# A two-layer transformer on one core: one list of rows per expert for a whole layer, 71 blocks in place of twice 39

## The reference, cut to what matters

```python
x = x + tanh(g_xattn[0]) * xattn0(layernorm(x), ctx)      # 8 heads of 64
x = x + tanh(g_ffn[0])   * ffn0(layernorm(x))             # silu(a)*b experts, with biases
x = x + tanh(g_xattn[1]) * xattn1(layernorm(x), ctx, ctx) # 16 heads of 8
x = x + tanh(g_ffn[1])   * ffn1(layernorm(x))             # gelu experts
# an expert layer: scores -> top 2 of 8 -> weights; y = sum of weight * expert(x) over the two
```

## Time and profile before

| | us |
|---|---|
| median of 3 runs | 836.9 (834.84 to 841.38) |
| span of the profiled execution | 772.1 |
| between that span and the median | 64.8 |
| granted TensorE clock, mean over the span | 0.945 |

### The profile page before, as it was taken

The page is one execution under the profiler, slowest core; times in us unless marked ns, Lnnn a source line. Parts: engine busy times, 40 slices in busy tenths (PEclk is TensorE's granted clock), DMA queues, the critical chain, the costliest instruction groups (busy, mean ns, idle before and its releaser), DMA issues.

```text
span 772.1 us, 17182 instructions
## 1 busy us (share of the span) xinstructions
PE 646.2 (84%) x4648; PEld 591.0 (77%) x4648; DVE 574.2 (74%) x2005; ACT 434.4 (56%) x1195; POOL 476.3 (62%) x693
## 2 busy tenths in 40 slices
PE   6889888988875789898978998898788875879896
PEld 5668777887765779888967787788788875868886
DVE  3369788988786678997977988987967753845763
ACT  2456565664444657666757776686566553434451
POOL 4034347776577777885563445675566577677771
PEclk9999999999798999999979999999999998999998
DMA  9646667544443235443713632532524013344646
GB/s 258 183 110 170 171 175 180 148 122 130 107 135 92 84 105 145 120 130 110 197 57 99 137 92 77 138 107 70 118 84 87 25 54 94 113 119 127 177 140 180
DMA packets 132633, 95.90 MB, mean 124 GB/s; under 512 B 32148, under 2 KB 120756, under 8 KB 132476
## 3 DMA queue, kind: packets, MB, share of 16 engines
q1 hardware_dynamic: 114844, 69.16, 35.1%
q0 software_dynamic: 9088, 19.68, 7.9%
q10 hardware_dynamic: 8608, 5.99, 2.7%
HBM read 55.09 MB, written 44.10 MB: 128 GB/s over the span
## 4 chain that ended last, share of the span: by engine, by line
PE 35%; DVE 28%; issue 11%; ACT 9%; POOL 8%; DMA 5%; SPq 2%; DVEq 1%; ACTq 0%; POOLq 0%
PE banks L1063 10%; PE banks L927 4%; DVE row_max L1297 4%; PE banks L1082 4%; DVE prob L1300 3%; POOL x_rows L1719 3%; DMA y_rows<-y_sb,result_at 3%; POOL y_rows L1726 2%; PE banks L809 2%; SPq L721 2%; PE banks L871 1%; DVE x_res L1569 1%; DVE row_sum L1351 1%; ACT xm L1177 1%; DMA v_rows<-vo 1%
## 5 line engine op out<-in xcount | busy, mean ns | idle before, releaser
L1726 POOL DMA_INDIRECT y_rows<-y_sb,result_at x156 | 151.4, 970 | 58.0 <-issue 31.2
L1063 PE MATMUL banks<-xb,up 128*128 128x128 f32 x936 | 140.2, 288 | 19.5 <-DVE hidden L1545 8.4
L1719 POOL DMA_INDIRECT x_rows<-xm,row x128 | 127.5, 996 | 34.9 <-issue 30.4
L1063 PEld LDWEIGHTS banks<-xb,up 128*128 128x128 f32 x936 | 122.0, 199 | 27.2 <-issue 10.6
L1082 PE MATMUL banks<-down,hidden 128*128 x624 | 99.8, 284 | 8.5 <-DVE y_sb L1562 8.2
L1681 POOL TENSOR_TENSOR v_flat<-v_raw,row_head 104x64 f32<-104x64 f32 (+1 forms) x128 | 55.8, 463 | 74.3 <-ACT v_raw L1219 73.8
L1082 PEld LDWEIGHTS banks<-down,hidden 128*128 128x128 f32 x624 | 85.0, 197 | 11.7 <-issue 11.1
L927 PE MATMUL banks<-v_flat,prob_t 128*128 128x108 f32 (+2 forms) x640 | 87.4, 286 | 3.1 <-issue 1.3
L927 PEld LDWEIGHTS banks<-v_flat,prob_t 128*128 128x128 f32 (+1 forms) x640 | 80.4, 199 | 10.8 <-ACT prob_t L1203 6.4
L1203 ACT ACTIVATE prob_t<-banks 128x512 f32<-128x512 f32 x192 | 72.7, 433 | 27.9 <-PE banks L894 26.9
L1297 DVE TENSOR_REDUCE row_max<-banks 128x8 f32<-128x616 f32 x96 | 75.5, 786 | 16.5 <-PE banks L886 9.6
(11 more groups left out here) (212 smaller groups left out, 1546.7 us busy)
## 6 DMA issues: line engine op xcount, KB each, us to landing
vo_flat<-v_rows SPq DMA_DIRECT2D x32, 256.0 KB
x_norm<-x_rows SPq DMA_DIRECT2D x86, 72.0 KB
x_far<-x_rows SPq DMA_DIRECT2D x70, 72.0 KB
v_rows<-vo SPq DMA_DIRECT2D x38, 128.0 KB
gathered<-y_rows ACTq DMA_DIRECT2D x32, 128.0 KB
q_rows<-up_raw SPq DMA_DIRECT2D x8, 512.0 KB, 2.8
q_even<-q_rows SPq DMA_DIRECT2D x12, 256.0 KB
q_odd<-q_rows SPq DMA_DIRECT2D x12, 256.0 KB
```

Of the source, the lines that this page charges most:

```text
L1063: done = pe.matmul(banks[:, UP_BANK[i % 2], part * P:(part + 1) * P], block_w[:, i % WR, part // 2, part % 2 * P:(part % 2 + 1) * P], xb[: ...
L1719: pool.indirect_dma_start(out=x_rows[i // HG][:, :], out_offset=bass.IndirectOffsetOnAxis(ap=row[:, n, c:c + 1], axis=0), in_=xm[:, i % 2, ...
L1726: pool.indirect_dma_start(out=y_rows[k][:, :], out_offset=bass.IndirectOffsetOnAxis(ap=result_at[:, i % (2 * YR):i % (2 * YR) + 1], axis=0 ...
```

## The change

The two lists per layer become one. Regions of `x_rows` hold a whole layer's rows (REGION = 32 x 128 + 128), there is one `x_rows` and one `y_rows` per layer, and LAYER_BLOCKS = (8192 + 8 x 127) // 128 = 71.

The blocks still start before the last group is ranked. PARTS = 2: the first table is made once five groups (20 tiles) are ranked and holds FIRST_BLOCKS = 40 - 7 = 33 blocks, which are surely full with these groups' rows. The second table, made when all eight are, holds the other 38: for each expert the begun rest of the first list, then its second list, 16 segments in place of 8. After FIRST_DONE = 40 + 7 = 47 blocks all rows of the first 20 tiles are computed.

```diff
+FIRST_GROUPS = 5
+PART_GROUPS = (FIRST_GROUPS, NG)
+LAYER_BLOCKS = (2 * NSEQ * P + NEXP * (P - 1)) // P
+SPARE = LAYER_BLOCKS - 2 * NSEQ
+FIRST_BLOCKS = 2 * GS * FIRST_GROUPS - SPARE
+FIRST_DONE = 2 * GS * FIRST_GROUPS + SPARE
+PART_BLOCKS = (FIRST_BLOCKS, LAYER_BLOCKS - FIRST_BLOCKS)
+AMONG = (16, GS * FIRST_GROUPS)
+LAST = NSEQ - AMONG[1]
-ON_PE = [1, 3, 5, 7, 9, 11, 13, 15]
+ON_PE = list(range(1, LAST, 2))
@@ expert_steps @@
-    for s in range(LAYER_BLOCKS + 4):
+    fetched = AHEAD
+    loads, combines = {}, {}
+    for b in range(AMONG[layer]):
+        begins = FIRST_DONE + 6 + (4 * b // 3 if layer == 0 else 11 * b // 10)
+        loads.setdefault(begins, []).append(("load", layer, b))
+        combines.setdefault(begins + 3, []).append(("combine", layer, b))
+    begin_after = max(combines) - len(after)
+    if layer == 0:
+        begin_after = min(s for s in combines if ("combine", 0, GS - 1) in combines[s]) - after.index([("norm", NG)])
+    for s in range(max(combines) + 1):
...
-        if AHEAD <= s + AHEAD < LAYER_BLOCKS:
-            step.append(("fetch", first + s + AHEAD))
+        for _ in range(2):
+            known = not tails and not any(t[0] in ("rank", "totals", "blocks") for t in late)
+            if fetched <= s + AHEAD and fetched < (LAYER_BLOCKS if known else FIRST_BLOCKS):
+                step.append(("fetch", first + fetched))
+                fetched += 1
...
-        if tails and not any(t[0] in ("rank", "totals") for t in late):
-            step.append(tails.pop(0))
-        b = (s - BLOCKS - 7) // 2
-        if s % 2 and 0 <= b < HT:
-            step.append(("load", layer, b))
-        if s % 2 == 0 and 0 <= b - 2 < HT:
-            step.append(("combine", layer, b - 2))
-        if s >= BLOCKS - 12 and after:
-            step += after.pop(0)
+        for _ in range(2):
+            if tails and not any(t[0] in ("rank", "totals") for t in late):
+                step.append(tails.pop(0))
+        step += loads.get(s, []) + combines.get(s, [])
+        if 0 <= s - begin_after < len(after):
+            step += after[s - begin_after]
@@ fetch, on SP @@
-                    w.wait_ge("tails", 16 * NEXP * (k + 1))
+                    w.wait_ge("tails", 16 * NEXP * (layer + k % PARTS))
                     for r in (0, 1):
-                        w.wait_ge(f"scattered{r}", 16 * HT * (k + 1))
+                        w.wait_ge(f"scattered{r}", landed(r, groups_of(k), 2) * 2 * GS)
@@ load, on ACT for tiles below AMONG[layer], else on SP @@
-                        w.wait_ge(f"y_out{r}", landed(r, BLOCKS * (k + 1), YR))
+                        w.wait_ge(f"y_out{r}", landed(r, blocks_of_tile(layer, b), YR))
@@ blocks, on DVE (second table: width 16, many 38) @@
-                    dve.tensor_reduce(block_e[:, k, :], passed[:, :, :], AX.X, ALU.add).then_inc(sem("table_step"))
+                    dve.tensor_tensor(base[:, 0:width + 1], (firsts if part else region)[:, 0:width + 1], since, ALU.subtract).then_inc(sem("table_step"))
+                    dve.tensor_reduce((segment[:, 0:many] if part else block_e[:, k, 0:many]), held, AX.X, ALU.add).then_inc(sem("table_step"))
+                    dve.tensor_tensor(delta[:, 0:width], base[:, 1:width + 1], base[:, 0:width], ALU.subtract).then_inc(sem("table_step"))
+                    dve.tensor_tensor(held, held, delta[:, 0:width].unsqueeze(1).to_broadcast(over), ALU.mult).then_inc(sem("table_step"))
```

More of the change, by code:

```diff
@@ L113, in route_tasks @@
             at.setdefault(u + step, []).append((kind, layer, g))
[L114 to L118, removed]
+            if kind == "rank" and g + 1 in PART_GROUPS:
+                part = PART_GROUPS.index(g + 1)
+                at.setdefault(u + step, []).append(("totals", layer, part))
+                for e in range(NEXP if part == PARTS - 1 else 0):
+                    at.setdefault(u + step + e // 2, []).append(("tail", layer, e))
+                at.setdefault(u + step + 1, []).append(("blocks", layer, part))
                 if layer == 0:
-                    at.setdefault(u + step + 2, []).append(("block_bias", layer, g // HG))
+                    at.setdefault(u + step + 2, []).append(("block_bias", layer, part))
         for j, step in enumerate(steps_of[1]):
@@ L190, in attention1_steps @@
             step.append(("exp1", u))
[L191 to L194, removed]
+        later = NSEQ - AMONG[0]
+        if u % 2 and u // 2 < later:
+            step.append(("load", 0, AMONG[0] + u // 2))
+        if u % 2 == 0 and 0 <= u // 2 - 2 < later:
+            step.append(("combine", 0, AMONG[0] + u // 2 - 2))
         step += tasks.get(u, [])
@@ L333, in order @@
             begun += 1
-    out += [("spread", n) for n in ON_PE] + [("keep_busy",)] + [("load_last", q) for q in range(HT // 2)]
-    out += [("combine_last", n) for n in range(HT)]
+    out += [("spread", n) for n in ON_PE] + [("keep_busy",)] + [("load_last", q) for q in range(LAST // 2)]
+    out += [("combine_last", n) for n in range(LAST)]
     apart = {t[1:] for t in out if t[0] == "rest"}
@@ L619, in of_block, with groups_of, blocks_of_tile @@
         def of_block(i):
-            return i // LAYER_BLOCKS, i // BLOCKS, i % BLOCKS
+            layer, n = divmod(i, LAYER_BLOCKS)
+            part = int(n >= FIRST_BLOCKS)
+            return layer, PARTS * layer + part, n - part * FIRST_BLOCKS
+        def groups_of(k):
+            return k // PARTS * NG + PART_GROUPS[k % PARTS]
+        def blocks_of_tile(layer, b):
+            return layer * LAYER_BLOCKS + (FIRST_DONE if b < GS * FIRST_GROUPS else LAYER_BLOCKS)
         def hiddens(n):
@@ L641, in last_done @@
                 return "last_act", ON_PE.index(n) + 1
-            return "last_dve", 2 * [m for m in range(HT) if m not in ON_PE].index(n) + 2
+            return "last_dve", 2 * [m for m in range(LAST) if m not in ON_PE].index(n) + 2
         def last_tile(n):
-            c = 2 * NSEQ - HT + n
+            c = 2 * NSEQ - LAST + n
             return x_res[:, c - NSEQ, :], token_w[:, :, c:c + 1]
```

281 lines of the change are left out of this document (165 added, 116 removed).

## The result

The kernel before took 835.9 us (median of 4, 834.3 to 841.4), the changed one 812.6 (810.0 to 816.7): a ratio of 0.9711, 95% interval 0.9672 to 0.9751, or 23.3 us less. The forecast was 823.4 us, 13.5 less, in a range from 814 to 835.

The account below looks back on a forecast made before the run. No engine was taken to bound the whole: POOL's stores bound layer 1's expert stage, PE and DVE pace layer 0's. Terms summed to -13.5 us, from the 836.9 us median to 823.4 us, range 814 to 835.

Parts of the forecast that it names:

- working base: Whole kernel: profiled span 772.1 us, with 64.8 us up to the median of 836.9 taken as unchanged by the change.
- (a): Layer 1's expert stage: 71 blocks, not 78; seven stores at 1.26 us of POOL's bounding queue, -8.8 us.
- (b): Layer 1's combines: twenty instead of sixteen and closer together, DVE's deficit against its lead; +1.0 us (0 to +3.4).
- the ring: Rival, chance 0.10: three gather buffers make ACT's gathers wait for combines in layer 1; +17.3 us at 5.7 us landings, 840.7 us.
- (c): End of kernel: twelve tiles instead of sixteen after the last store, two fewer copies out of PE; -1.4 us (-2.8 to 0).
- (d): Layer 0's expert stage: 71 blocks, sixteen combines packed closer; seven blocks at DVE's 1.22 us, -8.5 us.
- (e): Layer 0's first gather: ACT waits for a block's store two places nearer than before; +1.0 us (0 to +2.5).
- (f): Nine memsets of v_flat and k_diag move eight steps earlier, where POOL is still behind; 0 us (0 to +2).
- (g): Block tables cost DVE more: +1.2 us in layer 0's expert stage, +2.0 in both attention stages, hidden in layer 1's expert stage.
- (h): Costed at nothing: fewer SP tail writes, later fetches of layer 0's first block and block 33, stores beside block copies.
- full pace: Rival, chance 0.17: layer 0's seven blocks each return 1.83 us, tables and gathers hide; -22.0 us, 814.9 us.
- DVE as the bound of both layers: Rival, chance 0.23: DVE paces both expert stages, layer 1 loses 7.4 us, layer 0 returns only 6.7; -2.0 us, 834.9 us.

Follow-up runs that it names:

- the doubled blocks: Changed kernel with each layer's last seven blocks run a second time, 78 a layer; three runs: ratios 1.0055, 1.0006, 1.0051 to the kernel before.
- the last two runs: Both kernels unchanged, on a chip of the slower kind: kernel before 839.3 us, changed kernel 814.1 us, ratio 0.9693.

## Why the prediction was wrong

*The working base failed*: "64.8 us lie between it and the median of 836.9. I take these as unchanged." They lay inside the span: 837.0 us of time came with 835.2 of span on such a chip. The profile on record agrees stage by stage with the one taken on a quicker chip (130.1 and 111.7 us for 129.0 and 111.7), so it was of such an execution, though its chip is not on record; and nearly all of the missing time, 61.3 us, was that of the very blocks the change removes. The step that failed is "I take these as unchanged": by the table the 64.8 us shrank by 9.2, which takes 823.4 to 814.2, at the range's edge. Of the other 1.6, 1.0 is the median of before, 835.9 with its fourth run for 836.9.

*The terms of the change were right in sum* for the kernel that the profile showed: -13.4 (-9.8 to -16.6) measured, -13.5 forecast. That it meets to 0.1 is luck, since several terms were off and cancel.

(a) Layer 1's seven stores: the doubled blocks cost 1.2 us each for 1.26. Held there; with (b) the stage gave back 6.9 (111.7 to 104.8) for 7.8. On the chip on record POOL is not the bound, and they return 1.6 each.

(b) Closer combines +1.0: spreading them gave nothing back (104.9 us for 104.4). The waits that the term reckons with are there, but stay in front of POOL. ACT's wait at the first gather grew from 3.08 to 5.5 us, by the two places. The ring did hold ACT: six of its gelus stood behind a gather that waited for a combine, 6.0 us together, a wait that the profile of before does not have. DVE's own waits for landed stores shrank from 25.3 to 14.3 us, so the lead that the term speaks of paid for it, and POOL's queue lost next to nothing. The combines themselves waited 2.0 us for their gathers. The combines in the quicker chip's profile, what DVE waited for before them, and ACT's wait for the ring:

```profile
L1653 DVE SCALAR_TENSOR_TENSOR x_res<-gathered,token_w,x_res x104: 335/352/365, 351.0 to 743.1; 128x128 f32<-128x128 f32 x104
...
  DMA gathered<-y_rows: 2.0, 4
```

```profile
ACT hidden L1308 <- DVE x_res L1653: 6.0, 6, 1.9
```

(c) The end -1.4: about right for what it priced, but a wait came in that it did not have. From the first load of the last tiles to the end of the span the five profiles with sixteen tiles take 12.9 to 14.8 us (mean 13.4) and the eleven with twelve 10.7 to 12.0 (mean 11.4): 2.0 for four tiles, 1.6 without the 14.8. On the quicker chips the first of these loads comes 4.0 us after the last store, where before it came 759.10 - 756.66 = 2.4 after. It is not that combines or their stores to the output stand in its way: with sixteen combines among the blocks the last one ends 3.0 us before the last store starts, and the load still comes 4.0 after. What the load waits for is the landing of that last store. Of its sixteen landing signals fifteen stand within 2.2 us of its start, the last one at 3.8. In all six profiles with such a straggler (3.4 to 3.9 us) a load of instructions on queue q8, 0.9 to 1.4 us long, starts 1.0 to 1.8 us after the store; where none starts then, all sixteen have landed by 2.3 us, or by 2.8 with twenty widely spaced combines. That the two meet on one DMA engine is likely, but not tested. Net the end is -0.4 between the means of the two kernels' profiles on the quicker chips, and -1.0 on the slower, where the straggler is missing.

(d), (e) Layer 0: -6.3 by stage (129.6 to 123.3), as the forecast's -8.5 + 1.0 + 1.2, by two errors that cancel: seven blocks return 9.9 (133.2 - 123.3), and the rest of the change costs 3.7. The wait of (e) is there in both quick profiles of the changed kernel, 3.3 and 3.5 us, longer than the 2.5 allowed for it; but among the three with 78 blocks it is 3.2, 1.4 and 0.4, with stretches of 134.5, 132.6 and 132.6, so little of it reaches the stage. ACT's timeline on a quicker chip, the gather and the gate behind it:

```profile
345.51 0.36 ACTq L1316 DMA_DIRECT2D gathered<-y_rows  x1
345.97 0.63 ACT L1304 ACTIVATE gate<-banks,block_bias 128x128 f32<-128x128 f32 x2 [3.33 <-DMA y_rows<-y_sb,result_at]
```

A block returned more than DVE's 1.22: 1.4 to 1.5, PE's pace.

(f) held as far as can be told. (g) was too dear in the attention stages: +2.0 forecast, while on the slower chip the table's columns for them differ by 0.4 together (265.7 against 266.3 and 265.6; 251.6 against 251.6 and 251.9); on the quicker ones two profiles of one kernel differ by more. (h) held: no gap stands ahead of block 33's store on a quicker chip, in layer 1 it follows 1.26 us after the one before it. The other sign, stores of layer 1 more than 1.3 us apart before the last twenty, was badly chosen: early in the stage, where POOL still waits for DVE, stores stand further apart in the profile of before as well (1.77 us from the one before for its ninth, 2.41 for its eleventh).

The rival whose number came nearest, *full pace* with 814.9, was not what happened. It wanted 12.8 us from layer 0 and -22.0 on the kernel as profiled; layer 0 gave 6.3 and the whole 13.4. DVE as the bound of both layers and the ring as a bound fell as well.

The Trainium skill, SBUF — State Buffer, "SBUF: two separate sides", has the rule by which DVE's fp32 copies keep POOL from writing its descriptors and so would add to POOL's part of each block. In layer 1 of the quicker chip a 128x256 weight copy lay beside 47 of the 71 stores, the stores' median was 959 ns, with or without one, the one store of 1430 had no copy beside it, and a block cost 1.2 to 1.39 us and not the 1.55 of that rule. The trace does not bear it out for the stores here.

## What to carry to other kernels

Hold the profiled span against the timed runs before pricing anything: here the two differ by 1.7 to 2 us when they are of one execution, and a gap of 8% was time inside the kernel that the profile at hand did not show. Until it is placed, give the change a case in which this time sits in the stage that the change shortens. To price "so many units fewer", run the changed kernel with the units put back: it separates the number from everything else that came with it. And read the two sides by stage: a sum that meets can hold errors that cancel.

## What was not expected of the hardware

One program takes 772 to 775 us on four chips, and 836 to 839 where the result and the last two runs were taken; nearly the whole difference lies in two stages of it. Each experiment's runs were of one kind throughout; no chip was seen in both, and only one of the slow kind is known by its number. In these two stages the slower chip's profiles show engines that wait for PE's semaphore after its products are recorded as ended: in layer 1 of the changed kernel ACT alone ten times, up to 6.7 us, 37.9 together. The pauses come back at the same places: the one that ended at ACT's gelu at 710.28 ended at 711.22 in the second slow profile of the same kernel, and the slow profile of the kernel before has one for the same block 18, whose product ended at 713.93 and was copied by DVE at 720.59.

```profile
711.22 0.38 ACT L1308 ACTIVATE hidden<-banks 128x256 f32<-128x256 f32 x1 [6.16 <-remote]
```

The trace also keeps when each semaphore rose, and there the signals themselves are late. On a quicker chip each of PE's three semaphores of these stages rises 0.01 to 0.02 us after the product. In the pause above six rises, for products that were recorded as ended between 704.41 and 707.09, all stand between 710.20 and 710.44. Over layer 1's stores 115 of the 162 rises on record come more than 0.1 us after any product's end, against 0 of 189 on a quicker chip; over attention 1 it is 18 of 418, against 0 of 444. A burst closer together than the products speaks for signals that were held back rather than products that were late, but the ends of products are modelled, and that is an argument and no test.

For the changed kernel the queues that bring instructions moved the same amounts on both kinds of chip (0.62 and 0.43 MB), and the mean granted clock is only a little lower on the slower one (0.92 to 0.93 in its three profiles, against 0.94). What makes PE's signals late, and why so much less in the attention stages, stays open.
